# A decoder's cross attention: softmax sums from pairs of key tiles added by GpSimd and VectorE, one wait for a step's two exact scores, and a new order of the steps

## The chip, the cores and the metric

The kernel runs on one core of a Trainium2 chip. Its time is the device time of one launch in microseconds, the median of the runs; lower is better. TensorE is called PE, VectorE DVE, ScalarE ACT, GpSimd POOL and SyncE SP, as in the profile. SP issues nearly all DMAs.

## The reference, cut to what matters

A decoder of two layers over x of shape (8, 256, 512): each of six blocks is added to its input and normalized. The change touches only the stage that computes the last two, cross attention and the experts:

```python
# x: (8, 256, 512), ctx: (8, 256, 512); the 256 rows are channels, 512 are positions; 8 heads of 32 channels
qk = einsum('bhdq,bhdl->bhql', x_heads, ctx_heads) * 32 ** -0.5
x = layernorm(x + gamma * einsum('bhql,bhdl->bhdq', softmax(qk, axis=-1), ctx_heads).reshape(8, 256, 512))
gates = softmax(x @ Wr + br + bonus)                 # 8 experts
w = the two largest gates, divided by their sum, at their experts' places
h = relu(x @ Wd + bd)                                # 16 hidden units per expert
x = layernorm(x + sum over experts of w * (h @ Wu + bu))
```

## The kernel before, in words

The stages run one after the other. The last, `l1_cross_and_experts` (line 1799), starts at about 1633 us. Everything is float32, or float32 split into a high and a low part that are stacked along the contraction (`stack`, lines 1946 to 1957: 24 DMAs of 128 KB per batch).

**Units.** A batch has two halves of four heads each (T = 2, HT = 4). The scores are made twice. `rough_scores` (line 2348) makes them from the rounded high parts with queries on the partitions; VectorE's `maxima` (2205) takes each query's largest; `turn_largest` (2362) transposes these on TensorE, `round_largest` (2124) rounds them on ScalarE, and `place_largest` (1968) puts them as one more row below the stacked queries. `scores` (2369) then makes the exact scores, with the keys on the partitions and the largest subtracted by that row: one unit is one head and one tile of 128 keys, 16 units per half, numbered tile by tile, in each tile head by head. `exps` (2131) turns a unit's scores to a probability tile `pT` of 128x512 in a ring of NPT = 12. `values` (2379) takes a key tile's four units: four matmuls with the values into four column strips of `v_ps`, and four with a matrix of ones into `d_ps`, which give the softmax's sums. Each float32 matmul shows as two instructions in the trace.

**Steps.** All engines' programs are written out by hand over the same loop `steps()` (1882): 16 steps per batch, each with one pair of units. g counts the steps over all batches, from -11, as the rough scores run 11 steps ahead (LEAD). At each step every engine issues what the loop assigns to it, in order, with waits on semaphores between engines. TensorE's step g is rough scores of pair g + 11, then the exact scores of units 2g and 2g + 1, then `values` on odd g (two steps after its last exponential's scores), then what else stands at this step: `turn_hidden` at 0, `out` at 2, `turn_largest` at 5 and 13, `turn_context` at 7, `turn_x` at 10, `project` at 12 (lines 2434 to 2455). Before exact scores of unit u TensorE waits for the exponential of unit u - 2, which frees its PSUM bank. All other products share two PSUM tiles `a_ps` in turn (`slot_uses`, 1890): each user waits until the one before it on the same tile has been read.

**After a half.** `read_out` (2137) copies the sums and the values out of PSUM on ScalarE. For all but the last half the sums' inverses take a detour: `lay_sums` (1978) lays them over 128 partitions by DMA, `invert` (2214) takes reciprocals on VectorE, `keep_inverses` (1989) writes them to DRAM, `spread_inverses` (1993) reads them back spread to each head's 32 partitions. `residual` (2048) multiplies and adds on GpSimd, in two operations. Then `statistics`, `power`, `apply` normalize a batch, `turn_x`, `turned`, `project`, `shift`, `exponential`, `gate`, `choose`, `picks`, `weigh` make the experts' weights, `turn_hidden`, `hidden`, `out`, `add_experts` the experts' output, and `statistics`, `power`, `apply`, `store` end the batch.

**Start.** SP issues load(1) and gamma, then stack(0), next_load(2), residual(0) and the router's weights, and only then the loop. VectorE sets the row of ones in both `ks` (two memsets) ahead of its first `take_lo`, and waits for gamma.

Of the kernel before, what the change touches and what calls it, by code (L numbers as in the profile page):

```python
# [14 lines left out]
P = 128  # L15
B, S, D = 8, 256, 512
T = S // P
# [1775 lines left out]
NPT = 12  # L1793
# [5 lines left out]
def l1_cross_and_experts(core, ahead, x, ctx_in, y, sums, gamma, wr, br, wdn, bd, wup, bu):  # L1799
# [5 lines left out]
    with ExitStack() as ctx:  # L1805
# [12 lines left out]
        nbr = [sb(f"e_nbr{i}", [P, D], F32R) for i in range(2)]  # L1818
        pT = [sb(f"e_pT{i}", [P, D]) for i in range(NPT)]
        ones = sb("e_ones", [P, CX])  # L1820
        dsb = [sb(f"e_dsb{i}", [P, D]) for i in range(2)]
        vsb = [sb(f"e_vsb{i}", [P, D]) for i in range(2)]
        rcol = [sb(f"e_rcol{i}", [P, HT * D // P]) for i in range(2)]
        rec = [sb(f"e_rec{i}", [P, D]) for i in range(2)]
# [35 lines left out]
        s_mm, e_done, pv_mm, o_read, added5 = (s(n) for n in ("s_mm", "e_done", "pv_mm", "o_read", "added"))  # L1860
# [21 lines left out]
        def steps():  # L1882

            for b in range(-1, B + 2):
                for step in range(STEPS):
                    g = STEPS * b + step
                    if -LEAD <= g <= STEPS * (B + 1) + 6:
                        yield b, step, g

        def slot_uses(b, step, g):  # L1890
# [3 lines left out]
            if step == 0 and 0 <= b - 2 < B:  # L1894
                yield "turned", b - 2
            if step == 2 and 0 <= b - 2 < B:
                yield "out", b - 2
            if step in (5, 13) and 0 <= 2 * b + 1 + step // 8 < 2 * B:
                yield "largest", 2 * b + 1 + step // 8
            if step == 7 and 0 < b + 1 < B:  # L1900
                yield "context", b + 1
            if step == 10 and 0 <= b - 1 < B:
                yield "x", b - 1
            if step == 12 and 0 <= b - 1 < B:
                yield "hidden", b - 1
# [33 lines left out]
        with nc.Block() as block:  # L1939
            @block.sync  # L1940
            def _(sp):
# [26 lines left out]
                def place_largest(n):  # L1968
# [5 lines left out]
                    for j in range(HT):  # L1974
                        sp.dma_start(qs[b % 2][KX - 1:KX, t, j, :].bitcast(F32),  # L1975
                                     nbr[n % 2][j * CX:j * CX + 1, :].bitcast(F32)).then_inc(biased, 16)

                def lay_sums(n):

                    sp.wait_ge(o_read, 2 * n + 1)  # L1980
                    if n >= 2:
                        sp.wait_ge(kept[n % 2], 16 * (n // 2))
                    for j in range(HT):
                        row = dsb[n % 2][j * CX:j * CX + 1, :]
# [8 lines left out]
                def spread_inverses(n):  # L1993

                    sp.wait_ge(kept[n % 2], 16 * (n // 2 + 1))
                    if n >= 2:
                        sp.wait_ge(scaled, n - 1)
                    src = sums[n]
                    sp.dma_start(rec[n % 2][:], bass.AP(tensor=src.tensor, offset=src.offset,
# [8 lines left out]

                load(1)
                sp.dma_start(gcol[:], gamma.partition_broadcast(P)).then_inc(g_loaded, 16)  # L2010
                stack(0)
                next_load(2)
                residual(0)
                with nc.allow_non_contiguous_dma(reason="rows of 8 router weights, once"):
                    sp.dma_start(wrd[:, :, 0:E], wr.rearrange("(k p) n -> p k n", p=P)).then_inc(w_loaded, 16)
                sp.dma_start(wrd[:, :, E:], wdn.rearrange("(k p) n -> p k n", p=P)).then_inc(w_loaded, 16)
                sp.dma_start(bias[:, 0, 0:E], br.partition_broadcast(P)).then_inc(w_loaded, 16)
                sp.dma_start(bias[:, 0, E:], bd.partition_broadcast(P)).then_inc(w_loaded, 16)
                sp.dma_start(wu[:], wup).then_inc(up_loaded, 16)
                sp.wait_ge(zeroed, 1)  # L2020
                sp.dma_start(bup[0:E, :], bu).then_inc(up_loaded, 16)
                for b, step, g in steps():
                    if step == 0 and 0 < b + 1 < B:
                        stack(b + 1)
                    if step in (2, 10) and 0 <= 2 * b - 1 + step // 8 < LAST:
                        lay_sums(2 * b - 1 + step // 8)
                    if step in (4, 12) and 0 <= 2 * b - 1 + step // 8 < LAST:
                        keep_inverses(2 * b - 1 + step // 8)
                    if step in (5, 13) and 0 <= 2 * b - 1 + step // 8 < LAST:
                        spread_inverses(2 * b - 1 + step // 8)  # L2030
                    if step in (6, 14) and 0 <= 2 * b + 1 + step // 8 < 2 * B:
                        place_largest(2 * b + 1 + step // 8)
                    if step == 6 and 0 <= b - 2 < B:
                        store(b - 2)
                    if step == 8 and 0 < b + 1 < B:
# [492 lines left out]
```

## Time and profile before

| | |
|---|---|
| median of 3 runs | 2101.18 us (2098.77 to 2101.21) |
| the profiled execution | 2102.42 us, span 2100.3 us |
| mean granted clock of PE over the span | 0.943 of full speed |
| busy in the span | PE 1864.2 us (89%), DVE 1145.9 (55%), ACT 851.1 (41%), POOL 331.6 (16%) |
| the changed stage | 1633 to 2100.3 us; first exact scores at 1671.57, last probability tile at about 2052 |

In the rows further down "busy" is the time in which an engine executes; a wait is idle time of the engine named first, put down to what released it. Times in the timeline are microseconds from the start of the span, the second number is the length of a merged row, and the idle time before the row stands in brackets. The ends of matmuls are modelled, so the distance between starts of rows is the better measure on PE.

### The profile page before, as it was taken

How to read it: one execution, taken by the hardware profiler on the slowest of the kernel's cores; microseconds unless marked ns; L12 is line 12 of the kernel's file. 1: busy time of each engine (PE TensorE's matmuls, PEld its weight loads, DVE VectorE, ACT ScalarE, POOL GpSimd, SP SyncE). 2: the span in 40 equal slices, each digit the busy share in tenths (PEclk: the TensorE clock that was granted, in tenths of full speed). 3: DMA queues.
4: the chain of work that ended last, by engine and by line, in shares of the span. 5: the costliest groups of instructions: out<-in, count | busy, mean ns of one | idle time of the engine just before them, and what ended most of it. 6: DMA issues, size and time to landing. Idle time of an engine off the chain costs nothing. (4 is left out here: it accounts for less than half of the span.)

```text
span 2100.3 us, 30928 instructions
## 1 busy us (share of the span) xinstructions
PE 1864.2 (89%) x11568; PEld 1425.5 (68%) x11568; DVE 1145.9 (55%) x2133; ACT 851.1 (41%) x2040; POOL 331.6 (16%) x414
## 2 busy tenths in 40 slices
PE   6979999999976799999999987899996498899994
PEld 5869998998964688888888876677774133333332
DVE  3446444444435565555555436788876535555543
ACT  2225333333323343333333214666674145555552
POOL 0000000000011112111111001333332212223211
PEclk9989999999988899999999998999998589999997
DMA  3122000000012221111110013000101644444400
GB/s 103 44 97 71 21 21 21 21 21 21 26 54 78 83 79 46 36 31 41 46 36 16 11 41 120 11 32 32 51 21 61 174 115 102 112 115 124 102 22 25
DMA packets 83664, 119.83 MB, mean 57 GB/s; under 512 B 15221, under 2 KB 31221, under 8 KB 83517
## 3 DMA queue, kind: packets, MB, share of 16 engines
q1 hardware_dynamic: 83516, 117.86, 19.5%
q8 instruction: 93, 1.52, 0.3%
q14 instruction: 55, 0.44, 0.1%
HBM read 75.42 MB, written 16.98 MB: 44 GB/s over the span
## 5 line engine op out<-in xcount | busy, mean ns | idle before, releaser
L2212 DVE TENSOR_REDUCE e_nbx<-e_a_ps 128x2 f32<-128x1024 f32 x128 | 153.2, 1214 | 103.0 <-PE e_a_ps L2358 102.9
L1164 PE MATMUL yp<-ccy,toep 128*128 128x288 f32 x640 | 181.8, 435 | 19.7 <-POOL ccy L892 13.6
L2135 ACT ACTIVATE e_pT<-e_s_ps 128x512 f32<-128x512 f32 x256 | 139.0, 597 | 126.7 <-PE e_s_ps L2376 123.8
L1442 ACT ACTIVATE p<-p,nb,rq 128x128 f32<-128x128 f32 (+1 forms) x256 | 136.9, 541 | 94.8 <-DVE nb L1539 94.8
L1164 PEld LDWEIGHTS yp<-ccy,toep 128*128 128x128 f32 x640 | 126.0, 205 | 55.7 <-POOL ccy L892 14.8
L80 PE MATMUL q_ps<-a_xt_hi,wq_hi 128*128 128x256 f32 x512 | 151.7, 296 | 4.2 <-DVE wo_lo L112 4.1
L82 PE MATMUL q_ps<-a_xt_hi,wq_lo 128*128 128x256 f32 x512 | 146.5, 286 | 0.0
L81 PE MATMUL q_ps<-a_xt_lo,wq_hi 128*128 128x256 f32 x512 | 146.3, 286 | 0.0
L1062 DVE SCALAR_TENSOR_TENSOR hm<-gu_ps,us_col,sg 128x256 f32<-128x256 f32 x88 | 42.3, 480 | 184.1 <-ACT sg L971 184.1
L514 ACT ACTIVATE ex<-ex 128x512 f32<-128x512 f32 x64 | 40.4, 632 | 213.8 <-DVE ex L567 213.8
L1399 POOL TENSOR_TENSOR p<-p,rs 128x512 f32<-128x512 f32 x64 | 94.2, 1472 | 195.5 <-DVE rs L1546 195.5
L2376 PE MATMUL e_s_ps<-qs,ks 97*128 97x512 f32 x256 | 108.5, 485 | 18.4 <-DMA qs<-e_xh 14.2
L971 ACT ACTIVATE sg<-gu_ps,gs_col 128x256 f32<-128x256 f32 x88 | 41.6, 473 | 189.8 <-PE gu_ps L82 189.7
L545 DVE TENSOR_TENSOR tl<-t_ps,th 128x512 fp32r<-128x512 f32 x64 | 44.3, 692 | 132.7 <-ACT th L506 132.7
L80 PE MATMUL o_ps<-wo_hi,th 128*128 128x512 f32 x256 | 106.7, 417 | 1.9 <-DVE tl L545 1.9
L80 PE MATMUL gu_ps<-m_xt_hi,wg_hi 128*128 128x256 f32 x352 | 100.3, 285 | 8.2 <-DVE m_xt_lo L1054 8.2
L231 POOL TENSOR_TENSOR n_rstd<-n_mv,eps 128x2 f32<-128x2 f32 x16 | 3.1, 197 | 634.2 <-DVE n_mv L225 634.2
L80 PEld LDWEIGHTS q_ps<-a_xt_hi,wq_hi 128*128 128x128 f32 x512 | 99.9, 195 | 4.7 <-issue 4.5
L81 PE MATMUL o_ps<-wo_lo,th 128*128 128x512 f32 x256 | 101.2, 395 | 0.0
L82 PE MATMUL o_ps<-wo_hi,tl 128*128 128x512 f32 x256 | 101.1, 395 | 0.0
L80 PE MATMUL gu_ps<-m_xt_hi,wu_hi 128*128 128x256 f32 x352 | 100.1, 284 | 0.0
L81 PEld LDWEIGHTS q_ps<-a_xt_lo,wq_hi 128*128 128x128 f32 x512 | 99.8, 195 | 0.0
(296 smaller groups left out, 4904.7 us busy)
## 6 DMA issues: line engine op xcount, KB each, us to landing
x_after<-n_r SPq DMA_DIRECT2D x16, 512.0 KB, 2.8
toep<-padded_kernels SPq DMA_DIRECT2D x32, 256.0 KB, 3.6
qs<-e_xh SPq DMA_DIRECT2D x64, 128.0 KB, 2.5
ks<-e_ch SPq DMA_DIRECT2D x64, 128.0 KB, 2.5
x<-in_x SPq DMA_DIRECT2D x8, 512.0 KB, 4.3
a_x<-in_x SPq DMA_DIRECT2D x8, 512.0 KB, 4.5
ring<-in_wqT SPq DMA_DIRECT2D x8, 512.0 KB, 4.6
ring<-in_woT SPq DMA_DIRECT2D x8, 512.0 KB, 3.8
```

The costliest lines, as they stand in the source:

```text
L80: pe.matmul(out, whi, xhi, start=start, stop=False)
L81: pe.matmul(out, whi, xlo, start=False, stop=False)
L82: return pe.matmul(out, wlo, xhi, start=False, stop=stop)
L545: dve.tensor_tensor(tl[:], t_ps[:], th[:], ALU.subtract).then_inc(tl_done, 1)
L971: act.activation(sg[:], gu_ps[n % 2][:, 0, :], ACT.Silu, scale=gs_col[:, j:j + 1]).then_inc(sg_done, 1)
L1062: dve.scalar_tensor_tensor(hm[:], gu_ps[n % 2][:, 1, :], us_col[:, j:j + 1], sg[:], ALU.mult, ALU.mult).then_inc(hm_done, 1)
L1164: last = pe.matmul(yp[:, lo % 2, 0:NCOL], toep[h % 2][:, (lo - li) * P:(lo - li + 1) * P], ccy[h % 2][:, li, 0:NCOL], start=(li == 0), sto ...
L1399: pool.tensor_tensor(tile, tile, r, ALU.mult).then_inc(pn_done, 1)
L1442: act.activation(p[n % 3][:, h, part[t]], p[n % 3][:, h, part[t]], ACT.Exp, bias=nb[i][:, t, h:h + 1], scale=rq[u][:, t:t + 1], accum_out= ...
L2135: act.activation(pT[u % NPT][:], s_ps[u % 2][:], ACT.Exp).then_inc(e_done, 1)
L2212: dve.tensor_reduce(heads, slot("pair", n)[:], AX.X, ALU.max, negate=True).then_inc(nb_done, 1)
L2376: pe.matmul(s_ps[u % 2][:], ks[b % 2][0:KX, t, j, k * P:(k + 1) * P], qs[b % 2][0:KX, t, j, :], start=True, stop=True).then_inc(s_mm, 1)
```

## The change

The sums are no longer made from each probability tile. GpSimd adds the tiles of the first two key tiles of a half, head by head, to `early`, and VectorE those of the last two to `late`; `sum_up` multiplies these four and four tiles by the ones. That is 8 matmuls for the sums of a half in place of 16. The ring of probability tiles gets one more (NPT = 13), and ScalarE waits for the adds too before it writes a tile again. For space, `nbr`, `dsb`, `vsb` and `rec` have one buffer in place of two. `scores` takes a step's pair: one wait for the two exponentials before, then both matmuls. The read-out is in two parts with a semaphore each, values first.

Many pieces change their step. `values` moves from odd to even g, one step later. On PE: `project` 12 to 0 of the next batch, `turn_hidden` 0 to 4, `out` 2 to 7, `turn_context` 7 to 9, `turn_x` 10 to 14. On ACT: `read_out` 2, 10 to 3, 11; `turned` 11 to 15; `exponential` 13 to 1 of the next batch; `hidden` 1 to 5; `apply` of the experts 5 to 10, of the attention 9 to 12; `round_hi` "xh" 10 to 12. On DVE: `invert` 3, 11 to 6, 14; `add_experts` and its `statistics` 3 to 8, the attention's `statistics` 8 to 10; `shift`, `gate`, `choose`, `picks`, `weigh` from 13 to 15 to 1 to 3 of the next batch. On POOL: `residual` 14 and 6 to 0 of the next batch and 8; `power` 4 to 9 and 8 to 10; `take_lo` "xl" 12 to 14. On SP: `lay_sums` 2, 10 to 4, 12; `keep_inverses` 4, 12 to 6, 14, behind `place_largest`; `spread_inverses` 5, 13 to 7, 15; `store` 6 to 11. At the start stack(0) comes first, load(1) and gamma after it, the other loads at g = -1, behind place_largest(0); the memsets of the rows of ones stand at g = -3 and 0.

The core of the diff:

```diff
-NPT = 12
+NPT = 13
...
                 def add_early(n, j):
+                    u = UNITS // 2 * n + j
+                    pool.wait_ge(e_done, u + HT + 1)
+                    if n:
+                        pool.wait_ge(d_mm, 2 * n - 1)
+                    pool.tensor_tensor(early[j][:], pT[u % NPT][:], pT[(u + HT) % NPT][:], ALU.add).then_inc(early_done, 1)
...
+                    if step in (4, 5, 12, 13) and 0 <= b < B:
+                        add_early(2 * b + step // 8, step % 2 * 2)
+                        add_early(2 * b + step // 8, step % 2 * 2 + 1)
...
                 def exps(u):
                     act.wait_ge(s_mm, u + 1)
                     if u >= NPT:
+                        n, k = divmod((u - NPT) // HT, NQ)
                         act.wait_ge(pv_mm, (u - NPT) // HT + 1)
+                        if k < 2:
+                            act.wait_ge(early_done, HT * n + (u - NPT) % HT + 1)
+                        else:
+                            act.wait_ge(late_done, HT * n + (u - NPT) % HT + 1)
...
                 def add_late(n, j):
+                    u = UNITS // 2 * n + 2 * HT + j
+                    dve.wait_ge(e_done, u + HT + 1)
+                    if n:
+                        dve.wait_ge(d_mm, 2 * n)
+                    dve.tensor_tensor(late[j][:], pT[u % NPT][:], pT[(u + HT) % NPT][:], ALU.add).then_inc(late_done, 1)
...
+                    if step in (7, 15) and 0 <= b < B:
+                        add_late(2 * b + step // 8, 0)
+                        add_late(2 * b + step // 8, 1)
+                    if step in (0, 8) and 0 <= 2 * b - 1 + step // 8 < 2 * B:
+                        add_late(2 * b - 1 + step // 8, 2)
+                        add_late(2 * b - 1 + step // 8, 3)
...
-                def scores(u):
+                def scores(g):
+                    for u in (2 * g, 2 * g + 1):
+                        b, t, k, j = unit(u)
+                        if k == 0:
+                            pe.wait_ge(stacked[j], 16 * 6 * (b + 1))
+                            pe.wait_ge(biased, 16 * HT * (T * b + t + 1))
-                    if u >= 2:
-                        pe.wait_ge(e_done, u - 1)
+                    if g:
+                        pe.wait_ge(e_done, 2 * g)
+                    for u in (2 * g, 2 * g + 1):
+                        b, t, k, j = unit(u)
                         pe.matmul(s_ps[u % 2][:], ks[...], qs[...], start=True, stop=True).then_inc(s_mm, 1)
...
                 def values(n):
...
-                    for j in range(HT):
-                        last = pe.matmul(d_ps[j * CX:(j + 1) * CX, :], ones[:], pT[(HT * n + j) % NPT][:], ...)
+                def sum_up(n, parts, done, first):
+                    pe.wait_ge(done, HT * (n + 1))
+                    if first and n:
+                        pe.wait_ge(d_read, n)
+                    for j in range(HT):
+                        last = pe.matmul(d_ps[j * CX:(j + 1) * CX, :], ones[:], parts[j][:], start=first, stop=not first, ...)
+                    last.then_inc(d_mm, 1)
...
-                    if g % 2 and 0 <= (g - 3) // 2 < T * NQ * B:
-                        values((g - 3) // 2)
+                    if g % 2 == 0 and 0 <= (g - 4) // 2 < T * NQ * B:
+                        values((g - 4) // 2)
+                    if step in (0, 8) and 0 <= 2 * b - 1 + step // 8 < 2 * B:
+                        sum_up(2 * b - 1 + step // 8, early, early_done, True)
+                    if step in (2, 10) and 0 <= 2 * b - 1 + step // 8 < 2 * B:
+                        sum_up(2 * b - 1 + step // 8, late, late_done, False)
...
                 def read_out(n):
                     act.wait_ge(pv_mm, NQ * (n + 1))
                     if n:
                         act.wait_ge(added5, n)
                     act.activation(vsb[:], v_ps[:], ACT.Copy, scale=gcol[:]).then_inc(v_read, 1)
                     act.wait_ge(d_mm, 2 * n + 2)
                     if n:
                         act.wait_ge(laid[(n - 1) % 2], 16 * HT * ((n - 1) // 2 + 1))
                     act.activation(dsb[:], d_ps[:], ACT.Copy).then_inc(d_read, 1)
```

## Rows read from the trace of the kernel before

**Rows 1.** Windows of the stage: busy us (and instructions) of PE, PEld, DVE, ACT, POOL; clock, DMA

```profile
1740.00:1790.00 50.00, 45.62 (x246) 18.25 (x244) 27.05 (x48) 27.74 (x50) 14.11 (x15) 0.94 0.42 106
```

**Rows 2.** Groups by line and shape, 1690 to 2050: count, busy us, mean ns, idle before

```profile
L2212 DVE TENSOR_REDUCE e_nbx<-e_a_ps 128x2 f32<-128x1024 f32 x111 | 133.3, 1213 | 91.7 <-PE e_a_ps L2358 91.6
...
L2055 POOL TENSOR_TENSOR e_vsb<-e_vsb,e_rec 128x512 f32<-128x512 f32 x14 | 17.9, 1280 | 132.9 <-DMA e_rec<-cross_sums 132.9
...
L1937 POOL TENSOR_TENSOR e_cl<-ring,e_ch 128x1024 fp32r<-128x1024 f32 x3 | 7.1, 2379 | 30.1 <-ACT e_ch L2115 30.1
...
L2145 ACT ACTIVATE e_vsb<-e_v_ps,e_gamma 128x512 f32<-128x512 f32 x15 | 10.5, 698 | 0.0
...
L2151 ACT ACTIVATE e_r<-e_r,e_nm,e_rstd 128x512 f32<-128x512 f32 x14 | 10.6, 806 | 5.8 <-POOL e_nm L2073 5.8
...
L2115 ACT ACTIVATE e_xh<-x 128x1024 fp32r<-128x1024 f32 x3 | 3.2, 1070 | 0.0
...
L2295 DVE TENSOR_TENSOR e_r<-e_a_ps,e_r 128x1024 f32<-128x1024 f32 x6 | 7.3, 1224 | 17.2 <-PE e_a_ps L2430 17.2
```

**Rows 3.** Waits, 1690 to 2050: engine line, releaser, us in total, times, longest

```profile
POOL e_vsb L2055 <- DMA e_rec<-cross_sums: 132.9, 14, 25.9
...
ACT e_pT L2135 <- PE e_s_ps L2376: 99.1, 66, 3.6
...
PE e_a_ps L2366 <- DVE e_nbx L2212: 9.7, 5, 4.7
...
PE e_a_ps L2420 <- DVE f_hw L2288: 5.6, 6, 1.4
```

**Rows 4.** Timeline of PE: start us, us of the merged row, engine, line, operands

```profile
1852.94 0.50 PE L2358 MATMUL e_a_ps<-e_ch,e_xh 32*128 32x512 f32 x2
...
1854.04 1.07 PE L2388 MATMUL e_v_ps<-e_pT,e_vt 128*32 128x512 f32 x8
...
1854.92 1.05 PE L2391 MATMUL e_d_ps<-e_pT,e_ones 128*32 128x512 f32 x8
...
1855.90 0.49 PE L2358 MATMUL e_a_ps<-e_ch,e_xh 32*128 32x512 f32 x2
```

**Rows 5.** Timeline, two steps without a value block between them

```profile
1846.14 0.73 PE L2376 MATMUL e_s_ps<-qs,ks 97*128 97x512 f32 x2
...
1847.48 0.96 PE L2376 MATMUL e_s_ps<-qs,ks 97*128 97x512 f32 x2
...
1847.93 0.19 PEld L2376 LDWEIGHTS e_s_ps<-qs,ks 97*128 97x128 f32 x1 [0.30 <-issue]
```

**Rows 6.** Timeline, an inversion that waits, and what follows it

```profile
1836.61 0.25 DVE L2221 RECIPROCAL e_rcol<-e_rcol 128x16 f32<-128x16 f32 x1 [4.51 <-DMA e_rcol<-e_dsb]
...
1838.09 0.63 PE L2366 MATMUL e_a_ps<-ident,e_nbx 128*128 128x128 f32 x4 [2.53 <-DVE e_nbx L2212]
...
1841.98 1.93 PE L2388 MATMUL e_v_ps<-e_pT,e_vt 128*32 128x512 f32 x8
```

**Rows 7.** Timeline, one VectorE operation beside a GpSimd multiply and alone

```profile
1865.29 1.28 POOL L2055 TENSOR_TENSOR e_vsb<-e_vsb,e_rec 128x512 f32<-128x512 f32 x1 [8.00 <-DMA e_rec<-cross_sums]
...
1865.67 0.91 DVE L2262 TENSOR_TENSOR f_tsum<-f_top 128x2 f32<-128x2 f32 x1
...
2049.82 0.14 DVE L2262 TENSOR_TENSOR f_tsum<-f_top 128x2 f32<-128x2 f32 x1
```

**Rows 8.** Timeline, the start of the stage

```profile
1638.33 3.47 DVE L2298 MEMSET ks<- 1x4096 f32 x1 [0.80 <-DMA e_gamma<-in_gamma]
...
1642.98 1.22 DVE L1937 TENSOR_TENSOR e_xl<-x,e_xh 128x1024 fp32r<-128x1024 f32 x1
...
1664.87 2.48 SPq L1975 DMA_DIRECT2D qs<-e_nbr  x4
...
1671.57 1.19 PE L2376 MATMUL e_s_ps<-qs,ks 97*128 97x512 f32 x2 [14.23 <-DMA qs<-e_xh]
```

**Rows 9.** Timeline, the reciprocal of the last half batch

```profile
2062.06 3.32 DVE L2218 RECIPROCAL e_rec<-e_dsb 128x512 f32<-128x512 f32 x1
```

More of the change, by code:

```diff
@@ L2007, in next_load @@
                     load(b)
+                stack(0)
                 load(1)
                 sp.dma_start(gcol[:], gamma.partition_broadcast(P)).then_inc(g_loaded, 16)
[L2011 to L2021, printed above, removed]
-                for b, step, g in steps():
+                for b, step, g in steps():
+                    if g == -1:
+                        next_load(2)
+                        residual(0)
+                        with nc.allow_non_contiguous_dma(reason="rows of 8 router weights, once"):
+                            sp.dma_start(wrd[:, :, 0:E], wr.rearrange("(k p) n -> p k n", p=P)).then_inc(w_loaded, 16)
+                        sp.dma_start(wrd[:, :, E:], wdn.rearrange("(k p) n -> p k n", p=P)).then_inc(w_loaded, 16)
+                        sp.dma_start(bias[:, 0, 0:E], br.partition_broadcast(P)).then_inc(w_loaded, 16)
+                        sp.dma_start(bias[:, 0, E:], bd.partition_broadcast(P)).then_inc(w_loaded, 16)
+                        sp.dma_start(wu[:], wup).then_inc(up_loaded, 16)
+                        sp.wait_ge(zeroed, 1)
+                        sp.dma_start(bup[0:E, :], bu).then_inc(up_loaded, 16)
@@ L2034, in _ @@
+                    if step == 10 and 0 <= b and b + 3 < B:
+                        next_load(b + 3)
+                    if step == 11 and 0 <= b - 2 < B:
                         store(b - 2)
[L2035 to L2038 removed]
                 sp.wait_ge(stored, 16 * B)
@@ L2097, in _ @@
                         take_lo(pool, b + 2, "cl")
-                    if step == 12 and b + 2 < B:
+                    if step == 14 and b + 2 < B:
                         take_lo(pool, b + 2, "xl")
-                    if step == 14 and 0 <= b < B:
-                        residual(b, 0)
             @block.scalar
@@ L2195, in _ @@
                         round_hi(b + 2, "ch")
-                    if step == 9 and 0 <= b - 1 < B:
+                    if step == 10 and 0 <= b - 2 < B:
+                        apply(b - 2, nm6, nm6_done, rstd6, y6_done)
+                    if step == 12 and b + 2 < B:
+                        round_hi(b + 2, "xh")
+                    if step == 12 and 0 <= b - 1 < B:
                         apply(b - 1, nm5, nm5_done, rstd5, y5_done)
-                    if step == 10 and b + 2 < B:
-                        round_hi(b + 2, "xh")
-                    if step == 13 and 0 <= b - 1 < B:
-                        exponential(b - 1)
             @block.vector
```

178 lines of the change are left out of this document (90 added, 88 removed).

## The prediction

> **What bounds the kernel now.** I read the window view first, to find the stretch that the change touches: cross attention with the experts runs from 1633 us to the end, and in a window inside it TensorE is busy for 45.62 of 50 us, VectorE for 27.05, ScalarE for 27.74 and GpSimd for 14.11 [rows 1]. The reader is to see that TensorE bounds the stage and that the two engines that get new work have room on the average. The groups by line and shape then say what a unit costs [rows 2], and the waits say who holds TensorE up: VectorE's maxima delay turn_largest for 9.7 us in five waits, and weigh's output delays turn_hidden for 5.6 us in six [rows 3]. ScalarE waits 99.1 us for scores, so it has slack; GpSimd waits 132.9 us for the spread inverses [rows 3]. Last comes the timeline of a few steps, because the order inside a step decides here, not the shares.
>
> From the timeline a step without other work is 1.10 us of rough and exact scores (1852.94 to 1854.04); a value block takes 0.88 us (1854.04 to 1854.92) and the block of sums behind it 0.98 us (1854.92 to 1855.90) [rows 4]. There are 128 steps and 64 such pairs of blocks.
>
> **The sum block.** Before, each of the 64 value blocks is followed by a block of sums. After, there are two for each of 16 half batches, 32. TensorE loses 32 x 0.98 = 31.4 us of work [rows 4]. As it is the bound, this is the saving, if nothing else is late in its place.
>
> **The adds.** GpSimd gets 64 adds of 128x512 at 1.28 us [rows 2], 82 us, where it now waits longer than that; VectorE gets 64. No VectorE add of two such SBUF tiles is in the stretch; VectorE's take_lo of 128x1024 takes 1.22 us [rows 8], so half of it, an estimate of 0.61, and no less than nothing and no more than one GpSimd add (1.28) on top when the two meet. VectorE's share rises from 27.05 to about 32 of 50 us, still below TensorE. The adds are free only where their position lets them be. GpSimd's stand at steps 4, 5, 12 and 13; the ring of 13 probability tiles wants them from unit 13 on, the second exponential of step 6. In front of them is residual of step 0 or 8 and, at step 12, take_lo (2.4 us) [rows 2]. I put them at nothing and price the opposite as a rival. VectorE's collide twice:
>
> At step 8 VectorE now has add_experts (1.2), its maximum (1.21) [rows 2], two adds (1.3) and statistics (about 1.5) in a row, and only then the maximum of step 9. turn_context of step 9 uses the other bank, so rough scores of step 10 wait for that maximum: add_experts can start 4.5 us into step 7, the maximum of step 9 ends some 6.2 us after step 8 begins, and TensorE has about 5 us of work until then. 1.3 us in each of six batches, +8 us.
>
> At steps 2 and 3 gate, choose, picks and weigh run while GpSimd adds early tiles. In the trace of before a VectorE operation on 128x2 that takes 0.14 us took 0.91 us when it fell on a GpSimd multiply, and ended with it (1865.67 + 0.91 = 1866.58, against 1865.29 + 1.28 = 1866.57) [rows 7]. weigh then ends later than turn_hidden's place in step 4. Before, that wait is 5.6 us in six [rows 3]; I take 0.8 us more per batch, +5 us (bounds: nothing, and four adds of 1.28 each time, +31).
>
> The Trainium skill, "SBUF — State Buffer", section "SBUF: two separate sides", says that a VectorE operation with two SBUF inputs and a GpSimd operation that reads SBUF exclude each other for the whole instruction. The trace agrees in the pair of 0.14 and 0.91 us. By the rule alone each of 64 VectorE adds could wait one GpSimd add, 64 x 1.28 = 82 us on VectorE, an estimate that would still leave it below TensorE's share. The sum above doesn't use it.
>
> **One wait for two scores, values on even steps.** Today the first score of a step waits for the first exponential of the step before, the second for the second. A step with one wait starts when both are done. From the start of one step's scores to the load of the next weights that a second exponential released: 1846.14 to 1847.93, 1.79 us [rows 5]. TensorE's own work between two steps' scores is 1.10 us on an odd step, which now has no value block behind it, so 0.7 us of waiting appear in each odd step with nothing else in it (1, 3, 11, 15; the others hold turn_largest, out or turn_context). 4 x 8 x 0.7 = +22 us. Against it: today's odd steps spend 0.96 us on their scores instead of 0.73, and start them 0.1 us late (1847.48) [rows 4, 5]; about five per batch, 40 x 0.3 = -12. Net +10. The bounds are -12 (the wait is always over by then) and +22. An even step (1.10 + 0.88 = 1.98 us) covers the 1.79.
>
> **ScalarE's order.** read_out stays 1.3 us (0.698 for the values, and some 0.6 for the like copy of the sums) [rows 2], at steps 3 and 11. At step 12 round_hi "xh" (1.07) and apply (two of 0.806, 1.5 together) now follow each other [rows 2]: 2.6 us between the exponentials of step 12, already 0.7 us late through read_out, and those of step 13. With one wait, TensorE can't put a score of step 14 ahead of them. Step 12 then takes 0.4 us and step 13 2.0 us more than TensorE's work: 2.4 x 7 batches = +17. Before, apply and round_hi stood two steps apart and cost some 0.6 us of TensorE's time per batch, -4. Net +13. Bounds: nothing, if the probability tiles and the next value block hide it, and +17.
>
> **Inversion and SP's queue.** lay_sums is queued behind the 24 DMAs of stack. VectorE waits in invert at steps 3 and 11 for their landing (4.51 us), the next maximum is late, and turn_largest waits 2.53 us; after it the value blocks ran at the lower level of the clock, 1.93 us where 1.06 stands elsewhere [rows 6, 4]. In the change lay_sums moves to 4 and 12, invert to 6 and 14, after turn_largest. keep and spread follow at 6 and 7, residual at 8; place_largest now comes ahead of keep, which puts 2.5 us of issues before it. The 9.7 us of waits [rows 3] go. Of what the lower level cost behind them I take 5 us (two or three stretches of about 2 us each). -15. Late next: place_largest, issued about 21.6 us into a batch and wanted at 23 to 25 us, at about nothing.
>
> **Start and end.** stack(0) starts at 1644.2, when VectorE's two take_lo end, held by a memset of 3.47 us at 1638.33, one like it before and the wait for gamma [rows 8]. These move away, and it starts about 6.5 us earlier. But load(1) now stands behind stack(0), and ScalarE's queue has round_hi of batch 1 before round_largest(0): load(1) issued near 1654, landed near 1659, scaled, rounded, round_largest near 1663, place_largest issued to 1665.7 instead of 1667.35 (1664.87 + 2.48) [rows 8] and with an emptier queue. First scores at 1668 to 1670 instead of 1671.57; the router weights land later and hold VectorE at g = 0, which gives some back. -3 us, bounds -6 and +3. In the tail, read_out of the last half waits for late adds (0.61 us) but has one sum block fewer before it, and the reciprocal of 3.32 us at 2062.06 [rows 9] comes after batch 6's gate work instead of behind its out: -1. project of the first batch leaves the full pipeline, and the last but one's stands in the tail beside read_out: -2.
>
> **Sum.** -31.4 (sums) - 15 (inversion) - 3 (start) - 3 (tail) + 10 (one wait) + 13 (ScalarE) + 8 (VectorE at step 8) + 5 (gate) = -16.4 us. The profiled execution took 2102.42 us (span 2100.3), so 2086.0; it stands 1.24 us above the median of the runs, and I forecast 2084.8, 2085. So the queue of an engine that is not the bound gives back more than half of what the matmuls save.
>
> **Rivals.** (a) The returned 36 us come at half size or less: the waits of steps 12, 9 and 4 overlap one another, since an engine late once is waited for once. For it: ScalarE waits 99.1 us and VectorE's waits cost TensorE little outside turn_largest [rows 3]. Against: the chain score, exponential, exponential, score is a fixed length. -16.4 - 18 = -34.4 us, 2067; all gone, 2049. (b) It ends slower: GpSimd is late. Its place is step 12, where take_lo and four adds, 7.5 us, start behind residual, power and the landing of the spread inverses. The ring has some 5 us of room (two steps); from 5 us of lateness in residual of step 8 on, ScalarE can't write unit 13 of the half, and TensorE stands. At 2 us for each of 16 halves +32, so +15.6 and 2117. For it: 132.9 us of waits for the landing [rows 3]; against: they are 14 waits and spread moves only two steps. (c) The clock: the odd steps' 0.7 us holes and the longer ones at 9 and 13 bring TensorE to the lower level more often, as the stall at 1838 did [rows 6]. There a pair of steps costs 3.6 + 2.0 us instead of 3.8 by the blocks' times at that level, 1.8 more; over sixteen more pairs +29, so +12.6 and 2114. It decides from nine pairs on. (d) The change saves the blocks but TensorE only waits instead: no change, a part of the forecast's upper edge.
>
> **How the numbers follow.** The forecast has 0.57 with its own range 2074 to 2099, (a) 0.27, (b) 0.08, (c) 0.08. The range of 8 in 10 reaches into (a) and to the upper edge of (d): 2058 to 2103. Faster by over 0.2% (0.2%, 4.2 us, is about what a measurement of this kernel can tell) is (a) and nearly all of the forecast, 0.79; within it 0.09; slower 0.12.
>
> **What would show it.** Right: 256 instead of 512 sum matmul instructions; scores 0.73 us a pair throughout; odd idle steps of about 1.8 us from score to score; no wait of turn_largest for maxima over 1 us; a wait of 1 us or more for rough scores of step 10; a step 13 of over 3 us; GpSimd about 82 us busier. Wrong: TensorE's waits for exponentials near zero (a); ScalarE waiting for early adds (b); the granted clock of the stage clearly below 0.94 [rows 1] (c). If the stage's windows still show turn_largest waiting, the inversion term was mis-sized.

## The result and the profile after

The changed kernel takes 2130.32 us (median of 4 runs, 2123.98 to 2135.04), the one before 2100.43: a ratio of 1.0141 [1.0111, 1.0171]. It is slower by 30 us, where 2085 was forecast and 2103 was the upper edge. Its profiled execution took 2127.72 us (span 2125.9), 25.3 more than that of before.

From the page:

```profile
span 2125.9 us, 30696 instructions
...
PE 1863.5 (88%) x11312; PEld 1431.8 (67%) x11312; DVE 1207.5 (57%) x2197; ACT 849.9 (40%) x2040; POOL 410.8 (19%) x478
```

The window that answers to [rows 1], and the inside of the stage, 1740 to 2010 us, which the experiments are compared in:

```profile
1740.00:2010.00 270.00, 229.31 (x1068) 96.78 (x1060) 174.75 (x275) 135.79 (x242) 119.12 (x112) 0.84 0.41 103
1740.00:1790.00 50.00, 41.90 (x197) 18.11 (x190) 31.73 (x48) 24.11 (x44) 22.73 (x19) 0.81 0.44 109
```

The same 270 us of the kernel before:

```profile
1740.00:2010.00 270.00, 251.24 (x1372) 102.40 (x1370) 149.69 (x267) 153.68 (x272) 75.89 (x83) 0.95 0.42 108
```

TensorE is busy for 22 us less of the 270, and at a mean granted clock of 0.84 instead of 0.95: it waits more, and what it does takes longer. The waits, 1690 to 2050, to read beside [rows 3] (us in total, times, longest):

```profile
POOL e_vsb L2058 <- DMA e_rec<-cross_sums: 149.8, 13, 14.9
ACT e_pT L2154 <- PE e_s_ps L2417: 142.3, 75, 5.8
...
PE e_s_ps L2417 <- ACT e_pT L2154: 22.1, 34, 1.4
...
PE e_a_ps L2468 <- DVE f_hw L2316: 17.2, 6, 4.3
...
PE e_a_ps L2395 <- DVE e_nbx L2232: 9.0, 14, 1.3
...
DVE e_rcol L2249 <- DMA e_rcol<-e_dsb: 5.1, 4, 4.1
```

turn_largest's 9.7 us are gone; turn_hidden's 5.6 us have become 17.2; and 22.1 us are new ahead of the exact scores. The reason for the 17.2 stands in the timeline of one step 4 (start us, us of the merged row, engine, line; the idle time before it and what ended it in brackets):

```profile
1877.94 4.99 POOL L2072 TENSOR_TENSOR e_early<-e_pT 128x512 f32<-128x512 f32 x4
...
1880.46 1.26 DVE L2294 CAST f_chosen<-f_index 128x4 f32<-128x4 uint32 x1
...
1881.75 1.23 DVE L2298 TENSOR_TENSOR f_pick<-f_numbers,f_chosen 128x32 f32<-128x32 f32 x1
1882.88 1.90 POOL L2048 TENSOR_TENSOR x<-x,e_scale 128x1024 f32<-128x1024 f32 x1
1882.90 1.90 DVE L2302 TENSOR_TENSOR f_share<-f_top,f_tsum 128x4 f32<-128x4 f32 x1
1884.91 0.19 DVE L2308 TENSOR_TENSOR f_pick<-f_pick,f_share 128x32 f32<-128x32 f32 x1
...
1885.89 0.46 PE L2468 MATMUL e_a_ps<-ident,f_hw 128*128 128x128 f32 x1 [3.29 <-DVE f_hw L2316]
```

Three operations of 128x4 and 128x32 follow each other in picks. Each takes as long as what is left of a GpSimd operation: the first two end with the third and the fourth add (1881.72 and 1882.98 against 1877.94 + 3 and 4 times 1.25), the third with scale_x (1884.80 and 1884.78). Over six batches f_pick has a mean of 1228 ns and f_share of 1108 (count | busy us, mean ns | idle before):

```profile
L2298 DVE TENSOR_TENSOR f_pick<-f_numbers,f_chosen 128x32 f32<-128x32 f32 x6 | 7.4, 1228 | 0.0
...
L2302 DVE TENSOR_TENSOR f_share<-f_top,f_tsum 128x4 f32<-128x4 f32 x6 | 6.6, 1108 | 0.0
...
L2294 DVE CAST f_chosen<-f_index 128x4 f32<-128x4 uint32 x6 | 4.8, 807 | 0.0
```

What TensorE does behind that wait, steps 5 to 7 of the same batch and where the level returns:

```profile
1890.57 1.22 PE L2417 MATMUL e_s_ps<-qs,ks 97*128 97x512 f32 x2
1891.72 1.94 PE L2429 MATMUL e_v_ps<-e_pT,e_vt 128*32 128x512 f32 x8
...
1895.33 1.91 PE L2477 MATMUL e_a_ps<-f_wu,f_hwT 128*128 128x512 f32 x2
1897.03 1.91 PE L2478 MATMUL e_a_ps<-f_bu,f_wT 128*128 128x512 f32 x2
...
1900.03 1.02 PE L2478 MATMUL e_a_ps<-f_bu,f_wT 128*128 128x512 f32 x2
...
1902.07 1.06 PE L2429 MATMUL e_v_ps<-e_pT,e_vt 128*32 128x512 f32 x8
```

A value block takes 1.94 us at the lower level (1.2 GHz) and 1.06 at the upper one (2.4 GHz), a product of out 1.91 and 1.02. Ahead of this stretch TensorE had stood 3.29 us at turn_hidden.

### The profile page after: what moved, and what is told of

Read it like the earlier page. It is cut to its first block and busy times, and to the rows that moved or that the text cites. A ratio compares the mean times of both kernels' runs of the same rounds, so it can differ in the third digit from the quotient of the medians.

```text
span 2125.9 us, 30696 instructions
## 1 busy us (share of the span) xinstructions
PE 1863.5 (88%) x11312; PEld 1431.8 (67%) x11312; DVE 1207.5 (57%) x2197; ACT 849.9 (40%) x2040; POOL 410.8 (19%) x478
## 5 line engine op out<-in xcount | busy, mean ns | idle before, releaser
L2395 PE MATMUL e_a_ps<-e_ch,e_xh 32*128 32x512 f32 x256 | 75.0, 588 | 32.7 <-DVE e_nbx L2232 16.1
L567 DVE TENSOR_SCALAR ex<-q_ps,bq_col 128x256 f32<-128x256 f32 x128 | 55.8, 477 | 81.4 <-PE q_ps L82 81.4
```

Source lines behind the costliest of these rows:

```text
L567: dve.tensor_scalar(ex[p % 2][:, h, :], q_ps[p % 2][:, h, :], bq_col[:, head:head + 1], 0.0, ALU.add, ALU.min).then_inc(mq_done, 1)
L2395: last = pe.matmul(bank[:, i, :], xh[b % 2][d, t, q * P:(q + 1) * P], ch[b % 2][d, t, :], start=True, stop=True, skip_group_check=True, ti ...
```

## Why a batch is longer

Steady batches first. By the starts of step 0 in the two timelines a batch takes (1976.22 - 1812.29) / 3 = 54.64 us after and (1962.74 - 1817.63) / 3 = 48.37 before, 6.3 more. TensorE's waits over these three batches, after:

```profile
PE e_s_ps L2417 <- ACT e_pT L2154: 10.5, 15, 1.4
PE e_a_ps L2468 <- DVE f_hw L2316: 9.8, 3, 3.3
PE e_a_ps L2395 <- DVE e_nbx L2232: 4.8, 7, 1.3
```

and before:

```profile
PE e_a_ps L2420 <- DVE f_hw L2288: 2.9, 3, 1.4
PE e_a_ps L2366 <- DVE e_nbx L2212: 2.7, 2, 2.5
PE e_a_ps L2358 <- DVE e_nbx L2212: 2.2, 5, 0.5
PE e_a_ps L2401 <- ACT e_r L2151: 2.1, 3, 1.0
```

25.1 us against 9.9, in a batch +5.1. Four sum blocks fewer, 4 x 0.98, are -3.9. From rough scores of step 5 to those of step 8 it is 13.9 us (1887.12 to 1900.98), where an experiment at the upper level (e1 below) took 8.4 (1876.68 to 1885.11): +5.4. The value and the sum block of step 0 take 1.72 and 1.95 us in place of 1.06 and 1.04, +1.6. Eight odd steps with scores of 0.73 us in place of 0.96 [rows 5] are -1.8. The sum is +6.4, against 6.3 measured. That it comes so close is partly luck: in the kernel before, too, each of these batches has a value block at the lower level (1.93 us at 1841.98, 1.94 at 1871.94 and at 1920.30), with its neighbours about 1.5 us a batch, which the sum doesn't take off.

My theory (theory A in what was expected of the runs) was therefore: GpSimd's adds shut out the short operations of picks, TensorE stands at turn_hidden, and the loss is that wait and, larger, the lower level behind it. The rivals: the one wait for two scores is the cause (the waits ahead of the scores are the largest of TensorE); VectorE or ScalarE have become the bound; the adds cost more than the matmuls they replace, wherever they stand.

## The experiments

**e1: GpSimd's early adds of step 4 behind weigh.**

```
+                    if step == 4 and 0 <= b - 2 and b < B:
+                        pool.wait_ge(hw_done, T * (b - 1))
                     if step in (4, 5, 12, 13) and 0 <= b < B:     # GpSimd: add_early
```

> The changed kernel with one wait added: GpSimd starts its early adds of a batch's first half only when weigh of the experts is done. Theory A (the adds, and scale_x behind them, shut out VectorE's small operations on two SBUF tiles, weigh ends 3.9 us late, TensorE waits 3.2 to 4.3 us at turn_hidden, and the lower clock level follows for steps 5 to 7): that wait falls below 1 us and steps 5, 6 and 7 take about 1.8, 2.0 and 4.5 us in place of 2.7, 3.7 and 7.4. 2.8 + 5.6 us in each of six batches, 50 us: about 2080. Rival B (the holes left by the one wait hold the clock down and cost the time): the wait at turn_hidden falls but the stretches at the lower level stay, 17 us at most: 2113. Rival C (delaying the adds makes the ring of probability tiles late): ScalarE waits for early_done and it is no faster than 2130.

Measured: 2094.31 us, 0.9962 [0.9938, 0.9986] of before, 36 us less than the change. The same step 4 of e1:

```profile
1873.90 0.16 DVE L2296 CAST f_chosen<-f_index 128x4 f32<-128x4 uint32 x1
...
1874.09 0.19 DVE L2300 TENSOR_TENSOR f_pick<-f_numbers,f_chosen 128x32 f32<-128x32 f32 x1
1874.20 0.15 DVE L2304 TENSOR_TENSOR f_share<-f_top,f_tsum 128x4 f32<-128x4 f32 x1
...
1875.48 4.99 POOL L2072 TENSOR_TENSOR e_early<-e_pT 128x512 f32<-128x512 f32 x4 [9.74 <-DVE f_hw L2318]
```

GpSimd waits up to 9.9 us for it and nobody misses the adds; TensorE's matmuls of turn_hidden wait for nothing. One wait of an engine with slack, no work removed, turns a loss of 30 us into a gain of 6. But the lower level did not go: the window has clock 0.82 (in the profiled execution, which took 2103.24 us, more than the nine others; over the span its clock is 0.924, and 0.937 in the execution of 2080.76 us), and later in the same batch

```profile
1893.74 1.95 PE L2442 MATMUL e_d_ps<-e_late,e_ones 128*32 128x512 f32 x8
1895.62 0.79 PE L2397 MATMUL e_a_ps<-e_ch,e_xh 32*128 32x512 f32 x2
```

shows it after the 1.31 us hole at step 10, and again after one of 1.37 us at step 14. The hole at turn_hidden was one place of several. The length of the hole alone doesn't say where the level falls: the change has the like holes of 1.32 and 1.38 us, and the value blocks behind them (at 1908.38 and 1918.35) take 1.06 us.

**e2: the scores' two waits as before.**

```
-                    if g:
-                        pe.wait_ge(e_done, 2 * g)
                     for u in (2 * g, 2 * g + 1):
+                        if g:
+                            pe.wait_ge(e_done, u - 1)
```

> The changed kernel with the exact scores' waits as before the change: first score after the exponential two units earlier, second likewise. Theory A: only the scores' waits of about 0.5 us at steps 2, 4, 12 and 0 shrink, and part of the 1.4 us at step 14; the wait at turn_hidden stays at 3.2 us or more and steps 5 to 7 stay at the lower clock level: 1.5 to 2 us per batch, 2115 to 2120. Rival B (the holes hold the clock down): the lower level goes too, and the time falls by 40 us or more, to 2090 or below.

Measured: 2127.35 us, 1.0128 [1.0082, 1.0173]. The waits of e2:

```profile
PE e_a_ps L2468 <- DVE f_hw L2316: 24.1, 6, 5.2
...
PE e_s_ps L2417 <- ACT e_pT L2154: 4.4, 5, 0.9
```

The 22.1 us ahead of the scores shrink to 4.4, and turn_hidden's wait grows from 17.2 to 24.1: TensorE comes earlier to the point at which VectorE is late. With the collision in place the form of the wait is worth 3 us, and the intervals of e2 and of the change overlap: TensorE's largest wait was not the one that cost.

**e3: TensorE kept busy ahead of turn_hidden's wait** (three 128x512 products into the bank that it is about to fill; their results are not used).

```
+                    for _ in range(3):
+                        pe.matmul(bank[:, 1, :], core.ident[:], wu[:], start=True, stop=True, ...)
                     pe.wait_ge(hw_done, T * b + T)
```

> The changed kernel with three dummy products of 128x512 (float32, results not used) put into the PSUM tile of turn_hidden before it waits for weigh, about 2.6 us of work at the upper clock level in a wait of 3.3 us. It changes no dependency, only what TensorE does while it waits. If the clock's lower level after that wait is what costs (5.6 us in each of six batches by steps 5 to 7), those steps run at the upper level and the time falls by about 30 us, to 2100. If the level is set by something else (the smaller holes, other engines), nothing falls and it is 2130 or a few us more.

Measured: 2119.24 us (2103.67 to 2127.16 in 10 runs), 1.0078 [1.0045, 1.0112]. 11 us of the 30 go although no wait ends sooner. The clock of the window stays at 0.84: the value block of step 14 takes 1.94 us in e3 (at 1863.80) and 1.06 in the change (at 1863.69), and from there to step 0 the lower level stands, while behind turn_hidden only steps 4 and 5 are freed of it. This is seen in one execution, of 2126.34 us. The ten fall apart by their clock over the span: three took 2103.67 to 2104.68 us at 0.938 or 0.939, seven 2115.06 to 2127.16 at 0.925 to 0.934. What the filler did in the three was not profiled.

**e4: the change without the adds.** The sums are again four matmuls per key tile behind the values; one wait, the new order of the engines and the moved inversions stay.

```
-        add_early (GpSimd), add_late (VectorE), sum_up, and ScalarE's waits for them
+                    for j in range(HT):
+                        last = pe.matmul(d_ps[...], ones[:], pT[(HT * n + j) % NPT][:], ...)
```

> The changed kernel with the sums taken as before the change: four products with the ones behind each value block, no adds on GpSimd or VectorE, all other pieces in the new order and with one wait. TensorE has 31 us more work. Theory A: weigh is no longer shut out by adds (scale_x can still meet it), the wait at turn_hidden falls to 1 us or less and the lower level behind it goes: -50 + 31, about 2110, not above 2120. Rival D (the adds cost nothing, the new order of the steps is what is slow): turn_hidden waits as long as now and the time rises by the work, to about 2155 to 2160.

Measured: 2091.61 us, 0.9948 [0.9928, 0.9968]. Giving TensorE its 31 us of matmuls back makes the kernel 39 us faster than the change, and no wait of turn_hidden for weigh is left in its trace from 1690 to 2050. Its window:

```profile
1740.00:2010.00 270.00, 247.10 (x1396) 103.02 (x1388) 158.06 (x278) 156.51 (x279) 74.60 (x82) 0.96 0.43 108
```

It is as fast as e1 (2094.31), with more work at clock 0.96 against less at 0.82. So the rest of the change, without the adds, gains 9 us, where the sum's other terms give -16.4 + 31.4 - 5 - 8 = +2.

**e5: e1 with its holes filled** (products of 128x256, results unused: one in the rough scores of most even steps, three at step 14, three ahead of turn_context).

```
+                    if at > 20 and at % 2 == 0:
+                        for _ in range({14: 3, 6: 0, 8: 0, 10: 0}.get(at % STEPS, 1)):
+                            pe.matmul(bank[:, 0, 0:256], core.ident[:], wu[:, 0:256], start=True, stop=True, ...)
...
```

> The kernel whose GpSimd adds wait for weigh (2094 us), with dummy products (128x256 float32, about 0.43 us each at the upper level, results overwritten) where TensorE stands idle: one ahead of the rough scores of even steps other than 6, 8 and 10, three at step 14, three ahead of turn_context. No dependency is eased and TensorE has more work. Theory A+ (the lower clock level returns elsewhere when the wait at turn_hidden goes, because TensorE's holes are many and its work is less: granted clock 0.76 to 0.83 in that kernel against 0.94 before): the granted clock rises to 0.9 or more and the time falls, by about 15 to 25 us, to 2070 to 2080. Rival (the level isn't governed by TensorE's own activity, or the holes are too small to matter): clock as it was, time 2094 or up to 20 us more.

Measured: 2088.51 us, 0.9930 [0.9905, 0.9955].

```profile
1740.00:2010.00 270.00, 256.98 (x1362) 121.72 (x1354) 180.51 (x323) 158.24 (x285) 131.62 (x129) 0.97 0.43 109
```

The clock goes from 0.82 to 0.97, and the kernel's median is 5.8 us below e1's with work added and none taken away. So the lower level is a cost of its own; the gain is a third of what was expected, and small against the spread of e1 (the two intervals overlap). The fillers take time themselves, which was not measured apart.

**e6 and e7: the waits relaxed, with adds and without.** e6 is e1 with the scores' two waits, the experts' statistics at step 9 and round_hi "xh" at step 14; e7 is e4 with the same three.

```
-                    if step == 8 and 0 <= b - 2 < B:      # VectorE: statistics(b - 2, ...)
+                    if step == 9 and 0 <= b - 2 < B:
-                    if step == 12 and b + 2 < B:          # ScalarE: round_hi(b + 2, "xh")
+                    if step == 14 and b + 2 < B:          # behind apply of step 12
...                                                        # scores as in e2
```

> The kernel whose GpSimd adds wait for weigh, with the three other holes opened: two waits for the scores as before the change, the experts' statistics one step later behind the maximum (hole of 1.3 us at step 10), round_hi xh from step 12 to 14 (hole of 1.4 us at step 14). Theory A+: waits of TensorE fall by 4 to 5 us per batch and the lower level is met less: 2050 to 2070, below both kernels. Rival E (the adds in themselves leave TensorE so idle that the clock falls again at another place): the holes go, the granted clock stays at 0.8 and the time gets no lower than 2080.

> The same three changes in the kernel that takes the sums tile by tile on TensorE and has no adds (2092 us). If adds pay at last, this one is slower than e6_relaxed by up to 31 us of TensorE's work. If the adds cost more than they save even without holes, it is as fast or faster: about 2070 to 2080 from 2092, as it loses holes of 2 us in a batch.

Measured: e6 2079.22 us, 0.9889 [0.9865, 0.9912]; e7 2088.09, 0.9934 [0.9909, 0.9958]. With the places put right the adds are worth 9 us (no execution of either reaches the range of the other), not quite a third of the matmuls that they save. e6 still waits at one place:

```profile
ACT e_r L2173 <- POOL f_nm L2084: 22.8, 7, 9.7
```

**e8: one wait for two scores, alone, in the kernel before.**

```
+                        if g:
+                            pe.wait_ge(e_done, 2 * g)
                         scores(2 * g)
                         scores(2 * g + 1)
```

> The kernel before the change with one part of it: both exact scores of a step wait for both exponentials of the step before. By the length of the chain score, exponential, exponential, score (1.79 us) against 1.10 us of TensorE's work on a step without a value block behind it, it costs up to 0.7 us where such a step follows, less the 0.3 us that the second score no longer waits: 0.4 us in about five steps of each of eight batches, 10 to 20 us: 2110 to 2120. The rival, that one wait is free or gains through fewer waits, gives 2100 or less.

Measured: 2106.65 us, 1.0023 [1.0003, 1.0043], 6.6 us slower than before by the medians; the interval allows 0.6 to 9.

**e9: e6 with the experts' apply at step 13 instead of 10** (their store at 15, and the loop four steps longer for it), since GpSimd's factor for it comes late (the row of e6 above).

```
-                    if step == 10 and 0 <= b - 2 < B:     # ScalarE: apply(b - 2, ...)
+                    if step == 13 and 0 <= b - 2 < B:
...
-                    if step == 11 and 0 <= b - 2 < B:     # SP: store(b - 2)
+                    if step == 15 and 0 <= b - 2 < B:
```

> e6_relaxed (2079 us), with the experts' apply from step 10 to 13 on ScalarE and store from 11 to 15 on SP. In e6 ScalarE waits 22.8 us in seven for GpSimd's power at apply, and scores of step 12 wait 1.4 to 2.3 us for the exponentials behind it. If that wait is what is left on TensorE and drops the clock, it goes: 2 us of wait and 2 to 4 us of lower level in six batches, 2060 to 2070. If the lower level comes back elsewhere: 2075 to 2080.

Measured: 2066.51 us (2061.40 to 2070.00), 0.9815 [0.9765, 0.9865]: faster than before by 34 us and than the change by 64. Its window and two of its waits of 1690 to 2050:

```profile
1740.00:2010.00 270.00, 251.52 (x1300) 107.07 (x1296) 198.69 (x336) 163.11 (x297) 139.49 (x136) 0.96 0.43 109
```

```profile
ACT e_r L2173 <- POOL e_nm L2084: 9.6, 2, 9.4
...
PE e_s_ps L2419 <- ACT e_pT L2156: 2.6, 3, 1.7
```

**e10: e9 without GpSimd's wait for weigh**, e1's two lines taken out again.

> e9_apply_late without GpSimd's wait for weigh, so that early adds and scale_x fall on the gate's operations again. Theory A: turn_hidden waits 3 us or more and steps behind it run at the lower level; 5 to 8 us in each of six batches slower than e9, 2100 to 2110. If the other holes were the real cause and the collision only met them, it is within 10 us of e9.

Measured: 2101.39 us, 0.9998 [0.9977, 1.0019].

```profile
L2298 DVE TENSOR_TENSOR f_pick<-f_numbers,f_chosen 128x32 f32<-128x32 f32 x6 | 8.6, 1429 | 0.0
```

```profile
PE e_a_ps L2468 <- DVE f_hw L2316: 19.3, 6, 4.7
```

The collision is back and costs 35 us, all that e9 had gained: twice, in the change (36) and in the best version, with different surroundings.

**e11: e6 with all adds on VectorE**, the early ones at steps 4, 5, 12 and 13, and no wait of GpSimd.

```
-                        add_early(...)                    # GpSimd
+                    if step in (4, 5, 12, 13) and 0 <= b < B:      # VectorE
+                        add_early(2 * b + step // 8, step % 2 * 2)
```

> e6_relaxed with all adds on VectorE (early ones at steps 4, 5, 12 and 13) and no wait for weigh; GpSimd does none. By theory A the gate's operations meet only residual and scale_x, VectorE has 40 us more work of 0.61 us an add and stays below TensorE: 2060 to 2075, as fast as e9 or faster. If VectorE's queue becomes the bound, maxima come late, TensorE waits at rough scores and it is 2085 or more.

Measured: 2086.21 us, 0.9922 [0.9882, 0.9962]. No collision, but VectorE is busy for 214 of the 270 us and its maxima come late:

```profile
PE e_a_ps L2403 <- DVE e_nbx L2229: 9.7, 13, 1.4
```

e6 has 3.4 us of such waits. At the median e11 is 7 us slower than e6, but the intervals overlap, and it was not run with the apply of e9: that GpSimd is the better engine for half of the adds is likely, not shown.

**e12: the change with scale_x at step 8 instead of 6**, out of the way of f_share.

```
-                    if step == 6 and b + 2 < B:
+                    if step == (8 if b >= 1 else 6) and b + 2 < B:
```

> The changed kernel with one piece moved: scale_x from step 6 to step 8, behind residual, from batch 1 on. In its trace share, 0.16 us alone, takes 1.90 us beside scale_x, and the other operations of picks and weigh take 2 us more beside adds. So the wait at turn_hidden falls by about 1.7 us to 1.6 us, and the time by 10 us, or by up to 40 us if the shorter wait no longer brings the lower clock level: 2090 to 2120. If scale_x isn't what holds share, nothing moves: 2130.

Measured: 2135.66 us, 1.0157 [1.0107, 1.0208]; the intervals of it and of the change overlap.

```profile
PE e_a_ps L2395 <- DVE e_nbx L2232: 16.8, 15, 3.0
...
PE e_a_ps L2468 <- DVE f_hw L2316: 9.5, 5, 2.8
```

turn_hidden's wait nearly halves, and the waits for maxima rise from 9.0 to 16.8. The collision has only moved: at step 8 scale_x now meets VectorE's two late adds, which stand ahead of the maximum of step 9 and take 2.96 us where 1.28 was enough in the change, and rough scores wait 3.00 us (at 1912.61).

```profile
1906.92 1.89 POOL L2048 TENSOR_TENSOR x<-x,e_scale 128x1024 f32<-128x1024 f32 x1
1907.00 2.96 DVE L2240 TENSOR_TENSOR e_late<-e_pT 128x512 f32<-128x512 f32 x2
```

## Why the prediction was wrong, point by point

**The step that failed is the term "+5 us (gate)".** It saw the mechanism, with the right pair of rows [rows 7], and mis-sized it: "I take 0.8 us more per batch". It is the largest error of the sum; a second one, in the worth of the adds, stands in the ledger below. Undone by itself it measured 36 us (e1) and 35 us (e10 against e9). Two things were left out. First, the term added the new delay to the wait of before as if one operation met one add. picks is a chain of dependent short operations, and GpSimd's four adds and scale_x stand back to back: 1.1 + 1.04 + 1.75 us are lost in one pass (1.26, 1.23 and 1.90 against 0.16, 0.19 and 0.15), 3.9 in place of 0.8. The upper bound of +31 was built on four adds and would have been the better value. The Trainium skill, "SBUF — State Buffer", section "SBUF: two separate sides", says that whichever of the two operations starts first keeps the port for the whole instruction; the trace agrees for each of the three, with their ends within 0.1 us of the GpSimd operation's (f_share starts 0.02 us behind scale_x).

Second, the lower clock level behind a wait was in the sum only for the inversion that went away, and in rival (c) for the odd steps; the gate's longer wait had no such price. The level costs 5.4 + 1.6 us in each steady batch of the change, more than the 5.1 us of added waits. Two rivals named a slower kernel, (b) 2117 and (c) 2114, each with 0.08 and each still too fast; (c) had part of the mechanism. Its sign in the profile came out ("the granted clock of the stage clearly below 0.94": 0.84), its place only in part: in the change the longest stretch stands behind the hole at turn_hidden, which (c) doesn't name; in e1 the level stands behind the holes that follow steps 9 and 13, which it does.

**The ledger.** The runs divide the way from 2100.4 to 2130.3 us into three parts. All but the adds: -8.8 (e4), where the sum has -15 - 3 - 3 + 10 + 13 = +2. The adds when they keep clear of weigh: +2.7 (e1 against e4), where it has -31.4 + 8 = -23.4. The collision with weigh: +36.0 (the change against e1), where it has +5. So the collision was mis-sized by 31 us and the adds by 26; 11 us of luck in the first part hide some of it. The second failed step is therefore "As it is the bound, this is the saving, if nothing else is late in its place": TensorE's matmuls went, and nothing came back for them. Part of that is the lower level (5.8 us net in e5), and part are waits at other steps with what follows them (e6 gains 15 us on e1, e9 another 13). Term by term:

- Sum block, -31.4: 256 instructions instead of 512, as forecast. What TensorE loses in work became 9 us in e6 against e7, nothing in e1 against e4, and a loss of 39 in the change against e4. The adds' own price was put at nothing outside the two collisions.
- One wait, +10: 6.6 us alone (e8), 3 us in the change (e2). The holes were 0.51 to 0.58 us where 0.7 was said, ahead of the scores of steps 2, 4, 12 and 0, that is behind the odd steps that were named; scores took 0.73 us a pair, as said.
- VectorE at step 8, +8: the wait for rough scores of step 10 is 1.32 us in a batch; 1.3 was forecast.

```profile
1907.28 0.50 PE L2395 MATMUL e_a_ps<-e_ch,e_xh 32*128 32x512 f32 x2 [1.32 <-DVE e_nbx L2232]
```

- ScalarE, +13: the wait behind step 13 is 1.38 + 0.22 us, where 2.4 was forecast. Too large by a third.
- Inversion, -15: turn_largest's waits [rows 3, 6] are gone. e4 gains 8.8 us though one wait costs 6.6 (e8), which leaves -15.4 for all that is moved. The sum had -15 - 3 - 3 + 13 = -8 for it. By the interval of e8 that is 1 to 10 us better than forecast; which of the four it was, was not taken apart. ScalarE's is the one seen too large.
- Start, -3: first scores at 1667.61 us, where 1671.57 stands in [rows 8]; 1668 to 1670 was forecast.

```profile
1667.61 1.19 PE L2417 MATMUL e_s_ps<-qs,ks 97*128 97x512 f32 x2 [2.92 <-DMA qs<-e_nbr]
```

- Tail, -3: wrong. From the start of batch 7's step 0 to the end of the span it is 97.2 us (2125.9 - 2028.7) after and 90.2 before. Inside that stretch TensorE stands 2.77 us ahead of the scores at 2065.51, at the end of a chain that begins with VectorE's two late adds of step 8: beside residual they take 3.36 us instead of 1.28 (at 2056.74), the statistics and GpSimd's power come late, ScalarE's apply waits 1.87 us for them, and the exponentials stand behind it. This is one more meeting of adds that the sum had at nothing. The reciprocal [rows 9] is at 2082.98, 3.35 us.
- The adds' durations: GpSimd's 1.275 us, where 1.28 was forecast (busy 410.8 us, 79 more than before; 82 was said), VectorE's 0.68 where 0.61 was estimated.

**The rivals.** (a) is false as put: waits did not overlap to a gain, they added. (b) is false: ScalarE has no wait for early adds in the rows of 1690 to 2050, and GpSimd waits 149.8 us for the spread inverses. The collision was not GpSimd being late but GpSimd being busy. (c) in part, above.

**What stays open.** Within the change the wait and the level behind it were not separated by an experiment: e3 left the waits' ends and moved the level to other steps. How much of the 7 us in the tail is the level, and why e3 has executions at two clocks, 23 us apart, is open too. The windows' clocks of e1 and e3 come from one execution each. The gate's operations were kept out of the way by moving GpSimd; changing their operands so that they need not wait was not tried.

## What to carry to other kernels

Before a second engine gets work "into its slack", list every short dependent chain on VectorE that will now run beside GpSimd operations, and price each link at up to a whole GpSimd operation; then let GpSimd wait for the chain's end, if it is the engine with time, as here. When work is taken from TensorE, look for the places where it will stand for half a microsecond or more, and judge the change by busy time and granted clock together: 31 us of matmuls bought 9 us here once the holes were opened, and cost 39 before. Read the waits after each step, but don't take a row's size for its worth: the largest of TensorE in the change, 22.1 us ahead of the scores, gave 3 us when it went (e2), and the next, 17.2 us at turn_hidden, gave 36 (e1).

## What the runs showed of the hardware

- A cast of 128x4, one SBUF input and four elements per partition, takes 1.26 us beside a GpSimd add and 0.16 alone; not only operations with two inputs are shut out.
- With one hole filled, the lower clock level stood at other steps in the execution that was profiled (e3: clock 0.84 in the window, as without the filler); with many filled it went almost wholly (e5: 0.97). It comes in a batch in which no hole of TensorE is longer than 1.4 us (e1).
- With the clock at 0.82 in the window and 31 us less work e1 takes 2094 us, with 0.96 and the full work e4 takes 2092. TensorE's waits from 1690 to 2050 are alike in both (39 and 34 us by the rows of 1 us and more), so the level is the likely price; e5 gives back 5.8 us of it net of its fillers.
- A GpSimd add of 128x512 has a mean of 1275 to 1282 ns in the change, e1 and e9, while VectorE's has 0.68 us in the change, 0.72 in e1 and 0.89 in e9. Where these two kinds meet, it is mostly VectorE that pays. But it isn't always: where VectorE's adds start first, GpSimd's residual behind them pays (1.47 and, in the next operation, 1.60 us in place of 1.28 in e1, up to 1.81 at 1862.25).

```profile
1964.42 2.36 DVE L2242 TENSOR_TENSOR e_late<-e_pT 128x512 f32<-128x512 f32 x2
1964.77 1.47 POOL L2058 TENSOR_TENSOR e_vsb<-e_vsb,e_rec 128x512 f32<-128x512 f32 x1 [8.37 <-DMA e_rec<-cross_sums]
1966.31 1.60 POOL L2064 TENSOR_TENSOR e_r<-e_xr,e_vsb 128x512 f32<-128x512 f32 x1
```
